# Attention of a two-layer decoder on one core: scores of four strips in one visit, row maxima in another

## What is computed

```
x = x + attn(norm(x))         # a0: self-attention, rope on q and k, biases
x = x + entangled(norm(x))    # b0: one-head attention over a context
x = x + routed_ffn(norm(x))   # c0
x = x + attn(norm(x))         # a1: self-attention, no biases
x = x + xattn(norm(x), mask)  # a2: attention over a context, one mask, biases
x = x + ternary_ffn(norm(x))  # d1
```

```
scores = einsum('bhqd,bhkd->bhqk', q, k) * scale   # a2: where(mask, scores, -1e9)
probs = softmax(scores, axis=-1)
out = einsum('bhqk,bhkd->bhqd', probs, v) -> [b, s, 256] @ Wout + bout
```

## Time and profile before

| | us |
|---|---|
| median of 3 runs | 1377.79 |
| lowest and highest of them | 1377.32, 1381.33 |
| the profiled execution | 1381.43 |
| its span from first to last instruction | 1379.3 |
| PE busy | 1320.8 |
| DVE busy | 985.2 |
| ACT busy | 732.3 |
| POOL busy | 455.4 |
| a0, first PE product of the stage to last sum | 7.8 to 277.2 |
| a1 | 646.0 to 901.4 |
| a2 | 901.9 to 1204.5 |

### The profile page before, as it was taken

One profiled execution on the slowest core, in us unless ns is written; L12 is line 12 of the kernel. 1 busy time (PEld: TensorE's weight loads), 2 busy tenths in 40 slices (PEclk: granted clock), 3 DMA queues, 4 the chain that ended last, 5 costly groups with the idle time before them and its releaser, 6 DMA issues. The chain is left out here.

```text
span 1379.3 us, 41633 instructions
## 1 busy us (share of the span) xinstructions
PE 1320.8 (96%) x15764; PEld 1194.0 (87%) x15764; DVE 985.2 (71%) x2431; ACT 732.3 (53%) x1469; POOL 455.4 (33%) x550
## 2 busy tenths in 40 slices
PE   6999999999989999998999999989999999899997
PEld 5889999789979999998889988878888887689987
DVE  6888888656665455563777778667777778668885
ACT  3555555455654454552655566535555556356562
POOL 2212211123222121120000000046556655478884
PEclk9999999999999999999999999999999999899999
DMA  6000000031110000001000000020000000000000
GB/s 235 3 2 0 0 0 2 2 121 38 31 32 1 1 0 0 1 1 55 2 2 0 0 0 1 2 79 17 17 15 15 15 15 2 8 17 31 23 32 31
DMA packets 16772, 29.34 MB, mean 21 GB/s; under 512 B 3648, under 2 KB 7744, under 8 KB 16288
## 3 DMA queue, kind: packets, MB, share of 16 engines
q1 hardware_dynamic: 16672, 27.97, 6.2%
HBM read 23.77 MB, written 4.19 MB: 20 GB/s over the span
## 5 line engine op out<-in xcount | busy, mean ns | idle before, releaser
L891 DVE TENSOR_REDUCE a_row_max<-a_S 128x4 bf16<-128x512 f32 (+1 forms) x384 | 246.9, 683 | 50.6 <-PE a_S L1061 25.8
L784 ACT ACTIVATE a_probs<-a_S 128x512 f32<-128x512 f32 x384 | 209.0, 595 | 115.0 <-PE a_S L1074 59.4
L175 POOL TENSOR_TENSOR all_var_eps<-all_moments,all_ln_eps 128x2 f32<-128x2 f32 x96 | 25.0, 261 | 602.9 <-DVE all_moments L170 602.9
L1029 PE MATMUL a_S<-a_qm_hi,all_odd_split 32*128 32x256 f32 x1536 | 186.9, 301 | 7.2 <-DVE a_row_max L891 4.8
L746 POOL TENSOR_TENSOR a_shifts<-a_add_mask,a_row_max 128x512 bf16<-128x512 bf16 x128 | 134.9, 1070 | 116.3 <-DVE a_row_max L891 116.3
L1029 PEld LDWEIGHTS a_S<-a_qm_hi,all_odd_split 32*128 32x128 f32 x1536 | 131.2, 183 | 41.5 <-issue 25.3
L1020 PE MATMUL a_S<-all_odd_split,a_qm_hi 32*128 32x128 f32 x1536 | 126.8, 283 | 1.7 <-DVE all_odd_weights L1006 1.7
L1029 PE MATMUL a_S<-a_qm_lo,all_odd_split 32*128 32x256 f32 x768 | 108.1, 275 | 0.0
L1087 PE MATMUL a_AV<-a_probs,a_v_pad 128*32 128x128 f32 x3072 | 103.8, 276 | 0.0
L1020 PEld LDWEIGHTS a_S<-all_odd_split,a_qm_hi 32*128 32x128 f32 x1536 | 99.8, 185 | 2.7 <-DVE all_odd_weights L1006 2.5
L789 ACT ACTIVATE a_av_raw<-a_AV 128x512 f32<-128x512 f32 x96 | 57.6, 600 | 76.5 <-PE a_AV L1087 75.4
(11 more groups left out here) (263 smaller groups left out, 3833.7 us busy)
## 6 DMA issues: line engine op xcount, KB each, us to landing
all_cx<-in_ctx_turned SPq DMA_DIRECT2D x16, 256.0 KB, 2.7
all_cx<-in_ctx SPq DMA_DIRECT2D x16, 256.0 KB, 2.7
out_x<-all_x_res SPq DMA_DIRECT2D x16, 256.0 KB, 2.0
all_x_res<-in_x SPq DMA_DIRECT2D x7, 512.0 KB, 7.0
b_routed_wi<-in_L_ffn_wi_W SPq DMA_DIRECT2D x1, 1024.0 KB, 5.1
b_routed_wo<-in_L_ffn_wo_W SPq DMA_DIRECT2D x1, 1024.0 KB, 7.8
all_even_weights<-in_L_ffn_W_fc SPq DMA_DIRECT2D x1, 1024.0 KB, 5.0
all_even_weights<-in_L_ffn_W_proj SPq DMA_DIRECT2D x1, 1024.0 KB, 6.9
```

What stands on the lines that cost most here:

```text
L784: act.activation(probs[:, t % STEPS, :], S2[t % 2][:], ACT.Exp, scale=DH ** -0.5).then_inc(exp_ok, 1)
L891: dve.tensor_reduce(row_max[:, t % 4, :], S1[t % 2][:].rearrange("p (h k) -> p h k", h=QH), AXX, ALU.max).then_inc(max_ok, 1)
L1029: pe.matmul(S2[t % 2][:, c * HV * P:(c + 1) * HV * P], k[par][strip, c, tok], q[par][strip, c, b].rearrange("p h t -> p (h t)"), start=(c ...
```

## The change

The second scores and the max scores of a step no longer share a visit. What follows is per half group, that is, per sequence b.

- `scores(G, b)` writes the second scores of all four steps of the sequence, 24 products in the four strips in turn, into four banks.
- `maximum_scores(G, b)` writes the max scores of the four steps: 8 products that move 256 columns. Weights are now the plain high queries `q_hi`, and what moves is `km`, the high keys masked to one head each. Making `km` (two ACT instructions per group) and `q_hi` (one ACT instruction) is new.
- Banks 0 to 2 serve both kinds of scores; the fourth second scores have bank 3 and the fourth max scores bank 4. So max scores wait until the exponentials of three steps are taken, and second scores wait for all the maxima.
- Value products of both sequences share one bank, `AV`.
- Queries and keys are made for group G+2 in group G, values for G+1; the schedule starts at G = -2. The transposed x has two buffers in a0 and a1. `transposes` and `queries` share bank FA; `keys` and `values` share FB.
- In a1 the values are padded by DVE (`take_v`, now L1014), before by ACT.
- The weights' preparation for the next stage starts at other slots: the fold for b0 is in three pieces in the last two groups, the quantisation for the last stage is later in a2.

The core of the diff:

```diff
-    S1 = [nm.ps(f"S1_{i}") for i in range(2)]
-    S2 = [nm.ps(f"S2_{i}") for i in range(2)]
-    AV = [nm.ps(f"AV_{i}") for i in range(2)]
-    FA, FB = nm.ps("FA"), nm.ps("FB")
+    banks = [nm.ps(f"S{i}") for i in range(NQ + 1)]
+    S2 = banks[0:NQ]
+    S1 = banks[0:NQ - 1] + banks[NQ:]
+    AV, FA, FB = nm.ps("AV"), nm.ps("FA"), nm.ps("FB")
...
-                return pe.matmul(S1[t % 2][:, at * P:(at + 1) * P], qm_hi[parity][strip, c, b, v, :], k_hi[parity][strip, c, tok],
+                return pe.matmul(S1[j][:, c * HV * P:(c + 1) * HV * P], q_hi[strip, c, tok],
+                                 km[strip, c, b].rearrange("p h t -> p (h t)"), start=(not cross or c == 0), stop=not cross,
...
+            def maximum_scores(G, b):
+
+                if b == 0:
+                    pe.wait_ge(qhi_ok, G + 1)
+                    pe.wait_ge(km_ok, HV * (G + 1))
+                at_least(pe, exp_ok, step(G, b, -1))
+                at_least(pe, max_ok, step(G, b, 0))
+                for c in range(KC):
+                    for j in range(NQ):
+                        last = s1_pass(b, j, c)
...
+            def scores(G, b, par):
...
+                pe.wait_ge(max_ok, step(G, b, NQ - 1))
+                at_least(pe, exp_ok, step(G, b, 0))
                 for i in range(3 * KC):
...
+                    for j in range(NQ):
+                        s2_pass(b, j, par, i // 3, i % 3)
```

814 lines of the change are left out of this document (460 added, 354 removed).

## The result

| | before | changed |
|---|---|---|
| median, us | 1378.57 (6 runs) | 1403.33 (6 runs) |
| lowest and highest | 1376.73, 1381.33 | 1398.88, 1407.92 |
| span of the profiled execution | 1379.3 | 1402.9 |
| granted clock over the span | 0.985 | 0.977 |

The changed kernel takes 1.018 of the time before, with a 95% interval of 1.0154 to 1.0205: **slower by 25 us**. The forecast was 1373, with a range of 1354 to 1388; the kernel became slower instead of faster.

A forecast was written before the change was run, and what follows sets the result against it. PE's queue was taken to bound the repeated groups. Stage sums of +7.5 us (a0), -2.9 (a1) and about +0.5 (a2) saved together 5 us, taking the median 1377.79 to 1373, range 1354 to 1388.

The forecast's parts named there:

- The visits: Attention stages: a visit of 24 second scores takes 0.90 us, of 8 max scores 0.43; 0.94 us saved per group.
- The rival of strips that are not all at once: Four strips run below the rate of two and two, costing about 0.34 us a group: 1389 us, chance 0.13.
- shifts, turns, projections, value products and outputs keep their number: Repeated groups: only the score visits change PE's work, so the group's 0.94 us saving has no other product term.
- a0: Repeated groups of a0: 14.35 to 14.4 us each, 0.87 us saved per group, 12.2 us over 14 groups.
- The chain of DVE: a0's second half: `add_output` waits for output products and stands ahead of the maxima, priced at 0.1 us.
- a2: Repeated groups of a2: 17.0 us each, 0.78 us saved, with ACT sharing priced at 0.16; bounds 0.3 and 0.94.
- a1: `xT_lo`: a1: PE waits 0.7 us per group for `xT_lo` before queries, leaving about 0.20 of 0.94 saved.
- The starts: Schedule a group longer with no PE work added; filling the chain costs 2.5 us in a0, 2 in a2.
- The ends: Last four halves of each attention stage: PE work is shorter than the chain, 5.7 us of idle PE per stage.
- The chain priced at 6.8 us a half: One half's visit, turn, shift, exponentials, max visit and maxima sum to 6.8 us; PE waits where its work is less.
- the fold: a0's end: folding b0's weights, 5.2 us in three pieces, moves into idle halves and gives 3.5 us back.
- The clock: Rival: waits in each stage's last two groups lower PE's clock, costing 13 us: 1386 us; chance 0.12 with edges.

The follow-up runs named there:

- short maxima: The kernel before, with row maxima in the last two groups of each attention stage over the first 32 of 128 keys; a0's end 29.2 us against 31.0.

## Why the prediction was wrong

**The visits.** Right in size: 0.91 and 0.44. The reading was a little generous, since in the earlier trace rows the mixed visit has max scores in four of its six slots and not in all; that four strips of second scores run at the same rate was a guess that came true. The rival of strips that are not all at once is out. By the 3.07x of the Trainium skill (TensorE: Matmul & The Clock Gate, section Measured speedup vs the span model) a visit would have taken about 1.0 us, an estimate from that page; the measurement decides.

**The repeated groups: mis-sized.** The step that failed is the sentence that shifts, turns, projections, value products and outputs keep their number, and with it, unsaid, their price. Their number stayed; their price depends on the neighbours. In a group of a0 the visits gave 0.93 and the shifts 0.07, `transposes` 0.17; the turns took 2 x 0.13 of it back, the turns back 2 x 0.05, the output 0.09, projections 0.05 and the new wait for POOL 0.37. That leaves 0.30. No row shows a turn between a visit and shifts, or an output ahead of a visit. I should have put a bound on it.

**a0.** The chain of DVE was priced at 0.07 and was hardly a wait (two waits for row maxima in nine groups); instead the wait for POOL's low keys cost 0.30 to 0.37, a queue that the prediction did not walk: high keys stand on ACT behind four exponentials and the heads, low keys on POOL behind them. Measured 0.29 saved in a group, forecast 0.87.

**a2.** Measured 0.57, forecast 0.78. Besides the turns (0.26) there is a wait that the sum did not have: ahead of the max visits PE waits for ACT's third exponential, so that output and values take 1.77 to the next start instead of 1.60, about 0.3 in a group. Against it stands a gain that it did not have either: the shifts became 0.32 cheaper.

**a1: `xT_lo`.** Right in mechanism, place and size (0.7 forecast, 0.70 measured from start to start); with the turns and the output the group kept 0.03 of the 0.20 forecast.

**The starts: the largest miss per line of reasoning.** 4.5 us were given, 14.8 were measured. The sum called it a group more in the schedule "with no PE work added" and gave a flat amount. It did not follow DVE's queue there: statistics that wait for a load of x stand ahead of low parts (2.93), the norm and the mask ahead of the low context (3.22 and 1.78). Moving three lines gave back 4.8 and 3.0 us, of which 1.7 in a0 went with the clock.

**The ends.** For a1 the forecast of +5.7 was met by +5.6, which is luck twice over. The 5.7 does not come out of its own terms: four halves of 6.8 less work of 3.8, 3.8, 5.4 and 5.3 are 9 us, and 7.5 with the waits of the earlier trace rows taken off. And of the 5.6, 1.4 to 2.1 us are half clock: with none of it before the last output the end was 28.4 to 29.1 in four runs, +3.5 to +4.2. The chain priced at 6.8 us a half was 7.3 and 6.2. For a2, 8.7 was met by 9.6 with 5.7 us more of half clock in it. In a0 the fold should have given 3.5 us back by lying in idle halves. It did not:

```profile
273.08 1.89 PE L444 MATMUL a_FB<-all_even_weights 128*128 128x256 f32 x8
274.90 1.08 PE L1205 MATMUL a_AV<-a_probs,a_v_pad 128*32 128x128 f32 x32
275.92 1.99 PE L444 MATMUL a_S<-all_even_weights 128*128 128x256 f32 x8
...
278.18 1.84 PE L454 MATMUL a_S<-all_even_weights 128*128 128x1 f32 x16
...
282.32 2.93 PE L104 MATMUL a_FA<-all_odd_split 128*128 128x256 f32 x12 [2.02 <-DVE all_odd_split L976]
```

Its three pieces, 1.8, 1.8 and 1.7 us, stand right ahead of the last value products and behind them, not in the half before, where PE waited 2.77 at 266.06. The output waits 2.02 behind them and then runs at half clock. I had read the slots as a group earlier.

**The clock.** It was a rival with a price of 13 us and a chance of 0.12, and it is part of the truth: 24 us more at half clock in the starts and ends. What a microsecond of it costs, four pairs of stretches show: 1.3 us for 5.3 at a2's end, 1.7 for 6.8 at the end of a0 in the kernel before (31.0 and 29.2, if short maxima did nothing there), 2.5 for 5.8 in a half of a1, 2.3 for 4.9 at the start of the last stage. At 0.25 to 0.5 the 24 us are 6 to 12 of the 36 that starts and ends grew by, an estimate from these pairs. The rival's mechanism, that the waits bring the clock down, is not shown as a rule: of six executions with the same wait of 2.69 or 2.70 at a1's end, three had half clock beginning within about 1 us of its end, for 3.4 or 6.8 us, and three had none.

**The balance.** An estimate that is a difference of two numbers of 26 and 21 us needs a range from the error of each; I had taken one for the whole from the cases. Both numbers were off: the steady part gave 12 instead of 26, and starts and ends cost 36 instead of 21.

## What to carry to other kernels

Where PE is fully busy, price a moved product by its neighbours on both sides as well as by its kind: a block of whole-array float32 products cost 0.05 us more behind a strip visit, and 0.09 to 0.17 more ahead of one. A schedule that saves in the steady part is bought with longer starts and ends; for stages of 16 groups these cost three times what the steady part gained, so walk every queue through the first and last two groups before summing. Before an edit is given credit for a shorter start or end, look at the granted clock there in both runs. And apply such a change per stage: in the one stage without load waits, rope, mask and folded weights it gave 0.4% of the whole kernel once one line of DVE's order was moved; in the other two no run came out ahead.

## What the runs showed of the hardware

- Two fp32 normalise instructions of DVE, which read and write SBUF, took 2.57 us while POOL was at work on SBUF, and 0.73 when it was not. Row maxima and an addition that read PSUM kept their 0.68 and 0.69 us beside the same POOL instructions.
- Four strips with second scores ran at the rate of two and two: 24 products of 256 columns in 0.91 us.
- Four float32 transposes took 0.36, 0.44, 0.49 or 0.53 us to the next start, by what stood ahead of and behind them.
- A wait of 2.7 us on PE at the same place came with half clock in three executions and without it in three others, one of them with the same kernel ahead of it. A microsecond of half clock cost 0.25 us where PE mostly waited and 0.4 to 0.5 where it was busy.
